# Layer 2 image scores: from 96 small products of their own to four columns of the score products

## The reference

```python
q    = heads(x @ W_q);  k_t = heads(text @ W_k);  v_t = heads(text @ W_v)       # text: 252 tokens
probs_t     = softmax(q @ k_t^T * scale);  text_out = probs_t @ v_t
k_ip = heads(ip @ W_k_ip);  v_ip = heads(ip @ W_v_ip)                           # ip: 4 tokens
attn_scores = q @ k_ip^T * scale                                                # (16, 20, 256, 4)
qsem  = l2norm(probs_t @ text);  sem = qsem @ l2norm(ip)^T
fused = attn_scores + 0.5 * sem
ip_out = (softmax(fused) * spatial_mask) @ v_ip
out = (text_out + ip_out) @ W_out + b_out + x
```

## Time and profile before

| | us |
|---|---|
| median of 3 runs | 1647.1 |
| lowest, highest | 1647.05, 1652.91 |
| the profiled execution | 1653.22 |
| its span, first to last instruction | 1651.4 |

### The profile page before, as it was taken

One profiled execution on the slowest core, in us unless ns is written; L12 is line 12 of the kernel. 1 busy time (PEld: TensorE's weight loads), 2 busy tenths in 40 slices (PEclk: granted clock), 3 DMA queues, 4 the chain that ended last, 5 costly groups with the idle time before them and its releaser, 6 DMA issues.

```text
span 1651.4 us, 42229 instructions
## 1 busy us (share of the span) xinstructions
PE 1586.4 (96%) x14152; PEld 1411.9 (85%) x14152; DVE 1388.2 (84%) x4113; ACT 991.9 (60%) x2044; POOL 716.0 (43%) x629
## 2 busy tenths in 40 slices
PE   6999999999999999999999999999999999999986
PEld 6888888888888888778788999999999999999965
DVE  4688788888888888876879999999999999999985
ACT  3455555565655565554656666666666666666652
POOL 3234422222233322433556555555655555655441
PEclk9999999999999999997999999999999999999998
DMA  8334444443444444543233323332333323332211
GB/s 225 98 105 122 127 122 124 130 130 116 127 125 128 122 128 124 146 117 91 80 110 91 99 73 103 102 104 73 102 94 104 96 79 103 110 100 62 81 30 43
DMA packets 204224, 175.30 MB, mean 106 GB/s; under 512 B 45440, under 2 KB 203530, under 8 KB 204010
## 3 DMA queue, kind: packets, MB, share of 16 engines
q1 hardware_dynamic: 204010, 172.60, 36.3%
HBM read 112.13 MB, written 60.38 MB: 104 GB/s over the span
## 4 chain that ended last, share of the span: by engine, by line
PE 89%; DVE 5%; issue 2%; ACT 1%; DMA 1%; SPq 1%; DVEq 0%; POOL 0%; ACTq 0%; POOLq 0%
PE MISC L104 27%; PE GP L104 20%; PE NAT L287 10%; PE TR L300 8%; PE PV L346 5%; PE PV L331 4%; PE PV L328 3%; PE PV L349 2%; PE MISC L249 2%; PE MISC L390 1%; PE MISC L488 1%; DVE ZP L920 1%; DVE TMP L801 1%; PE MISC L389 1%; PE MISC L410 1%
## 5 line engine op out<-in xcount | busy, mean ns | idle before, releaser
L1013 POOL TENSOR_TENSOR ZS<-ZP 128x256 f32<-128x256 f32 x267 | 279.8, 1048 | 295.7 <-DVE ZP L920 294.0
L562 ACT ACTIVATE P<-TA 128x512 f32<-128x512 f32 x320 | 202.3, 632 | 280.7 <-DVE TA L913 279.3
L287 PE MATMUL NAT<-KS,QS 65*128 65x256 f32 x1280 | 300.5, 317 | 3.1 <-DMA KS<-qk_parts 1.6
L930 DVE SCALAR_TENSOR_TENSOR PM<-P,PH 128x512 f32<-128x512 f32 x320 | 269.1, 841 | 0.0
L104 PE MATMUL GP<-PH,GH 128*128 128x256 f32 (+1 forms) x960 | 249.1, 289 | 18.0 <-DVE ZP L920 16.1
L300 PE MATMUL TR<-QS,KS 69*128 69x256 f32 (+1 forms) x1280 | 260.4, 285 | 6.0 <-DMA QS<-max_rows 4.5
L805 DVE TENSOR_REDUCE MX<-NAT 128x2 f32<-128x504 f32 x320 | 216.0, 675 | 44.2 <-PE NAT L287 39.5
L287 PEld LDWEIGHTS NAT<-KS,QS 65*128 65x128 f32 x1280 | 201.5, 192 | 56.6 <-issue 41.9
L104 PE MATMUL GP<-PH,GL 128*128 128x256 f32 (+1 forms) x960 | 243.1, 281 | 0.0
L237 POOL TENSOR_TENSOR PARTS<-QKF,PARTS 112x508 fp32r<-112x508 f32 (+3 forms) x93 | 120.1, 1291 | 269.5 <-ACT PARTS L590 268.9
L565 ACT ACTIVATE P<-TR 128x512 f32<-128x512 f32 x320 | 192.5, 601 | 73.8 <-PE TR L300 70.8
(11 more groups left out here) (256 smaller groups left out, 3772.7 us busy)
## 6 DMA issues: line engine op xcount, KB each, us to landing
QS<-qk_parts SPq DMA_DIRECT2D x480, 64.0 KB
KS<-qk_parts SPq DMA_DIRECT2D x480, 64.0 KB
qk_parts<-PARTS SPq DMA_DIRECT2D x128, 224.0 KB, 2.9
CT<-in_ctx_t SPq DMA_DIRECT2D x32, 512.0 KB, 3.9
qk_parts<-PARTS SPq DMA_DIRECT2D x64, 192.0 KB, 2.4
XT<-in_x_t SPq DMA_DIRECT2D x48, 112.0 KB, 2.7
XT<-x_t SPq DMA_DIRECT2D x48, 112.0 KB, 2.3
XB<-in_x SPq DMA_DIRECT2D x16, 320.0 KB, 4.0
```

What stands on the lines that cost most here:

```text
L287: ins = e.matmul(NAT[s % 2][:, i * T:(i + 1) * T], QS[0:KQ, h, i * 128:(i + 1) * 128], KS[0:KQ, h, :], start=True, stop=True)
L562: e.activation(P[:, s % NP, :], TA[:, s % 2, :], ACT.Exp, scale=SCALE).then_inc(q["exp"], 1)
L930: e.scalar_tensor_tensor(PM[:, s % 2, :], P[:, (S1 + s) % NP, :], 2.0, PH[:, s % NS, :].bitcast(F32), ALU.mult, ALU.subtract).then_inc(q[" ...
L1013: e.tensor_tensor(ZS[s % NZ][:, :], ZP[:, s % 2, 0:S], ZP[:, s % 2, S:2 * S], ALU.add).then_inc(q["zs"], 1)
```

## The change

The image keys of the batch are copied by ACT from KIP into columns 252 to 255 of QKF and of PARTS's high part, two copies of 4 columns ahead of the two large ones, for each of the three channel groups. POOL subtracts over 512 columns in place of 508. The stacked keys therefore hold the image keys in the padding, and NAT holds the image scores in columns 252 to 255 of each half. ACT reads these 2 x 4 numbers of each partition out of NAT in every iteration from t = 310 on, scaled, into SC. PE waits for that read before it overwrites the bank. TR uses 124 key columns in its second half in place of 128, so the top partitions of that bank are set to zero once, in the last two steps of layer 1. Removed are the mask products on DVE, the six products and the scaling of slot 17, the mask's DMA, and the memset of the padding.

```diff
@@ PE @@
                 if s >= 2:
                     e.wait_ge(q["mx"], s - 1)
+                if s >= S1 + 2:
+                    e.wait_ge(q["sc"], s - S1 - 1)
                 for i in range(2):
                     ins = e.matmul(NAT[s % 2][:, i * T:(i + 1) * T], QS[0:KQ, h, i * 128:(i + 1) * 128],
                                    KS[0:KQ, h, :], start=True, stop=True)
...
-                w = TRK0 if b < B else TRK1
+                w, t1 = (TRK0, T) if b < B else (TRK1, NT)
                 for i in range(2):
-                    ins = e.matmul(TR[s % 2][:, i * S:(i + 1) * S], KS[0:w, h, i * 128:(i + 1) * 128],
+                    t_i = min((i + 1) * 128, t1)
+                    ins = e.matmul(TR[s % 2][0:t_i - i * 128, i * S:(i + 1) * S], KS[0:w, h, i * 128:t_i],
                                    QS[0:w, h, :], start=True, stop=True)
...
-                for i in range(2):
-                    for m, (_, mn) in enumerate(MT):
-                        w = mn // 4
-                        ins = e.matmul(k[:, i * 80 + m * 28:i * 80 + m * 28 + w], QKF[0:mn, m, i * 128:(i + 1) * 128],
-                                       KBD[0:mn, m, 0:w // 4, :], start=True, stop=True)
-                ins.then_inc(q["scm"], 1)
@@ ACT, after the exponential and PH of iteration t @@
+            s = t + LEAD - 1 - S1
+            if 0 <= s < S1:
+                b, h = divmod(s, H)
+                if s == 0:
+                    e.wait_ge(q["pv"], G1 - NGRP)
+                if h == 0 and b >= 3:
+                    e.wait_ge(q["fu"], 8 * (b - 3) + 2)
+                e.wait_ge(q["mx"], S1 + s + 1)
+                e.mul(SC[:, b % 3, :, NI * h:NI * h + NI], NAT[s % 2][:, :].rearrange("p (a t) -> p a t", a=2)[:, :, NT:T], SCALE).then_inc(q["sc"], 1)
...
+                        ip = KIP[0:mn, m, NI * (b - B):NI * (b - B) + NI]
+                        e.copy(QKF[0:mn, m, w:S + T], ip)
+                        e.copy(QKF[0:mn, m, 0:w], k[0:mn, 0:w])
+                        e.copy(PARTS[0:mn, m, 0, w:S + T], ip)
+                        e.copy(PARTS[0:mn, m, 0, 0:w], k[0:mn, 0:w]).then_inc(q["qk_hi"], 1)
...
-                e.mul(SC[:, b % 3, :, :], ring.bank["scm", b][:, 0:160].rearrange("p (a n) -> p a n", a=2), SCALE).then_inc(q["sc"], 1)
@@ DVE @@
-                e.wait_ge(q["sc"], b + 1)
+                e.wait_ge(q["sc"], H * (b + 1))
...
-                e.tensor_tensor(KBD[0:112, 0:2, :, :], KMASK[0:112, :, :].unsqueeze(1).broadcast_to([112, 2, 8, 4]),
-                                own[0:112, 0:2, :].unsqueeze(2).broadcast_to([112, 2, 8, 4]), ALU.mult).then_inc(q["kbd"], 1)
...
-                e.tensor_tensor(TA[:, s % 2, :], TR[s % 2][:, :], ST[:, b % 2, :], ALU.add).then_inc(q["sum"], 1)
+                ins = e.tensor_tensor(TA[:, s % 2, :], TR[s % 2][:, :], ST[:, b % 2, :], ALU.add)
+                if s >= S1 - 2:
+                    ins.then_inc(q["tail"], 1)
+                    e.wait_ge(q["tail"], s - S1 + 3)
+                    ins = e.memset(TR[s % 2][96:128, S:2 * S], 0.0)
+                ins.then_inc(q["sum"], 1)
```

More of the change, by code:

```diff
@@ L44 @@
 AT1 = dict(q=(0, 4, 9), k=(1, 5, 10), spill=(2, 6, 11), x_in=-22, xts=-9, c_in=-15, ctn=-4, cts=-2, v=(6, 8), gr=(12, 13), gl=(13, 14),
-           kbd=9, scm=17, vip_in=38, vip=46, cmb=48, rs=((48, 49, 50, 51, 52, 53), (48, 49, 50, 51, 52, 53)), inv=56, f0=60, f2=61, sub=64, tx=65, sum=68, f1=71,
+           vip_in=38, vip=46, cmb=48, rs=((48, 49, 50, 51, 52, 53), (48, 49, 50, 51, 52, 53)), inv=56, f0=60, f2=61, sub=64, tx=65, sum=68, f1=71,
            ptt=72, hst=(74, 76), htl=(75, 77), om=(78, 82), y=(79, 83), out=84, xb_in=66)
@@ L53 @@
 WO_IN, WO_HI, WO_LO = S1 + 28, S1 + 32, S1 + 33
-MASKS_IN, SMALL, PADS, SEL_IN = S1 - 21, S1 - 19, S1 - 30, S1 - 16
+MASKS_IN, SMALL = S1 - 21, S1 - 19
 ONES_OF = (S1 - 18, S1 + 2)
@@ L160, in build @@
         sb, pair = tiles(second)
-        PH, KMASK, KBD = sb("PH", [128, NS, 2 * S], F32R), sb("KMASK", [128, 8, 4]), sb("KBD", [128, 3, 8, 4])
+        PH = sb("PH", [128, NS, 2 * S], F32R)
+        sb("in_wvi0", [128, 128])
         VMASK, E21 = sb("VMASK", [80, C]), sb("E21", [128, SLOT])
@@ L235, in parts_low @@
     def parts_low(e, b, m):
-        mn, w = MT[m][1], S + T if b < B else S + NT
-        e.tensor_tensor(PARTS[0:mn, m, 1, 0:w], QKF[0:mn, m, 0:w], PARTS[0:mn, m, 0, 0:w].bitcast(F32), ALU.subtract).then_inc(q["qk_lo"], 1)
+        mn = MT[m][1]
+        e.tensor_tensor(PARTS[0:mn, m, 1, :], QKF[0:mn, m, :], PARTS[0:mn, m, 0, :].bitcast(F32), ALU.subtract).then_inc(q["qk_lo"], 1)
     @block.tensor
@@ L583, in _ @@
                             e.wait_ge(q["tl"], b)
-                        else:
-                            e.wait_ge(q["scm"], b - B)
+                        if b == B:
+                            e.wait_ge(q["once_s"], 2)
                     if b:
@@ L588, in _ @@
                     e.wait_ge(q["qk"], 3 * b + m + 1)
-                    e.copy(QKF[0:mn, m, 0:w], k[0:mn, 0:w]).then_inc(q["qk_f"], 1)
-                    e.copy(PARTS[0:mn, m, 0, 0:w], k[0:mn, 0:w]).then_inc(q["qk_hi"], 1)
+                    if b < B:
+                        e.copy(QKF[0:mn, m, 0:w], k[0:mn, 0:w]).then_inc(q["qk_f"], 1)
+                        e.copy(PARTS[0:mn, m, 0, 0:w], k[0:mn, 0:w]).then_inc(q["qk_hi"], 1)
+                    else:
+                        ip = KIP[0:mn, m, NI * (b - B):NI * (b - B) + NI]
+                        e.copy(QKF[0:mn, m, w:S + T], ip)
+                        e.copy(QKF[0:mn, m, 0:w], k[0:mn, 0:w])
+                        e.copy(PARTS[0:mn, m, 0, w:S + T], ip)
+                        e.copy(PARTS[0:mn, m, 0, 0:w], k[0:mn, 0:w]).then_inc(q["qk_hi"], 1)
             b = of1(t, AT1["sub"])
@@ L884, in _ @@
                                 RZ[:, :, :].unsqueeze(3).broadcast_to([128, 2, H, D]), ALU.mult).then_inc(q["tx"], 1)
[L885 to L893, removed]
-                e.tensor_tensor(KBD[0:112, 0:2, :, :], KMASK[0:112, :, :].unsqueeze(1).broadcast_to([112, 2, 8, 4]),
-                                own[0:112, 0:2, :].unsqueeze(2).broadcast_to([112, 2, 8, 4]), ALU.mult).then_inc(q["kbd"], 1)
-                e.tensor_tensor(KBD[0:96, 2, :, :], KMASK[0:96, :, :], own[0:96, 2, :].unsqueeze(1).broadcast_to([96, 8, 4]),
-                                ALU.mult).then_inc(q["kbd"], 1)
             b = of1(t, AT1["ctn"])
@@ L1048, in _ @@
             if b is not None:
+                if b == 0:
+                    e.wait_ge(q["w1_m"], 16)
                 e.wait_ge(q["vip_in"], 16 * (b + 1))
@@ L1076, in _ @@
                 e.tensor_tensor(WO[1][0:CK, :, :], WOR[1][0:CK, :, :], WO[0][0:CK, :, :].bitcast(F32), ALU.subtract).then_inc(q["w1_lo"], 1)
[L1077 to L1080, removed]
             if t == SMALL:
                 e.wait_ge(q["vm"], 3 * B)
-                e.memset(KBD[:, :, :, :], 0.0).then_inc(q["ready"], 1)
                 e.memset(E21[:, :], 0.0).then_inc(q["ready"], 1)
-                e.wait_ge(q["ready"], 2)
+                e.wait_ge(q["ready"], 1)
                 e.memset(E21[:, 21:22], 1.0).then_inc(q["ready"], 1)
@@ L1183, in _ @@
                 if b < 2:
-                    e.wait_ge(q["ready"], 4)
+                    e.wait_ge(q["ready"], 3)
                 if b:
```

5 lines of the change are left out of this document (1 added, 4 removed).

## The result

The changed kernel takes 1664.7 us (median of 4 runs, 1662.2 to 1669.6) where the kernel before takes 1650.0 beside it (4 runs, 1647.1 to 1654.0): ratio 1.0091, 95% interval 1.0055 to 1.0127, so 14.7 us slower. A later measurement of both gave 1.0098 (1.0075 to 1.0122). The profiled execution took 1669.62 us with a span of 1667.8, against 1653.22 and 1651.4 before: +16.4 us, where the prediction summed +15.

The account below looks back on a forecast made before the run. PE was taken to set the pace, DVE close behind. Steady batches +3.5, end of layer 1 +8 and first batches +3.5 summed to +15 us, giving 1662 us; range 1643 to 1676.

Parts of the forecast that it names:

- The mechanism: PE's next NAT waits for ACT's small read, queued behind the exponential and PH; 1662 us, chance 0.62.
- Rival B: Reads come early enough that PE never waits and DVE becomes the bound: 11.5 us less, 1636; chance 0.12.
- Rival C: Cheaper restart and ends, early batches absorb lateness: steady -2, early +1, end of layer 1 +4, 1650; chance 0.18.
- the end of layer 1: Iterations 311 to 319 take 2.8 us each through the new wait, delaying NAT of 321: +8 us, bounds +4 to +11.
- Rival D: Each small operation costs as much as the 160 column read, 0.30 us: steady +10, end +10, early +5, 1672; chance 0.08.
- The loop's links: TR to exponential 0.44 us, to PH 0.68, then 0.52, read 0.19, to PE 0.10: TR to NAT 1.93 us.
- Slot 17: Steady batch, where the products are removed: NAT waits for the read, so 0.39 us gained and not 1.36.
- Slot 2: Steady batch: exponential already late behind ACT's copies, tiny copies add 0.15 us; loss of 0.48 us with PE's restart.
- Slot 14: Short slot of a steady batch: read through at 1020.04 against NAT at 1019.97; loss of 0.1 us with the restart.
- The other slots: Remaining slots of a steady batch: covered by PE's own products, with 0.08 us loss for the closest.
- The first batches: Start of layer 2, short and long iterations alternate, late at 322, 342, 362: +3.5 us, bounds 1 to 6.
- The last iterations: End of the kernel: also has short iterations, but DVE's ZP holds them anyway; 0.

Follow-up runs that it names:

- the opened one: Changed kernel with ACT's small read placed ahead of the exponential instead of behind PH: 0.9944 of the kernel before, 1643.8 us.
- the doubled read: Changed kernel with a second small read of the same 8 columns, to a scratch tile, ahead of the real one: 1.0172 of the kernel before.
- the kernel with f1=70: Kernel before with one offset changed, DVE's two masked products issued in slot 10 in place of slot 11: 0.9964 of the kernel before.

## Why the prediction was right

**The mechanism: right.** The wait was where it was said, ACT's share of the chain rose, and taking the loop apart took the loss away (1.0098 to 0.9944). Rival B fell with the changed kernel and came true in the opened one. Rival C asked for cheaper ends; the end of layer 1 was dearer (+10.8 for its +4). Its steady part of -2 us was about as near to the measured 0 as my +3.5. Rival D fell with the doubled read.

**The loop's links.** TR to NAT measured 1.96 us for 1.93 + 0.03. The read lasts 0.171 us (0.19; my own slope gives 0.196), and from its start to NAT 0.32 us pass, as predicted for the two links with the start (0.19 + 0.10 + 0.03). I weighed the Trainium skill's 0.3 us budget (ScalarE: Activation LUTs, rules for kernel authors) and passed it over; the 0.171 us bear that out. The budget is given for an activation whose bias is a pointer operand, which I had left out. Another section of the Trainium skill's page (ScalarE: Activation LUTs, What ACT_TABLE_LOAD costs) has a fixed 186 ns for an activation with immediate scale and bias; with 8 elements that is an estimate of 0.19 us, which is closer. The Trainium skill lets successive activations overlap by about 93 ns. The trace agrees: the two reads above last 0.17 us each and start 0.07 apart, so they overlap by 0.10.

**The terms of the sum.**
- Slot 17: gain 0.39 predicted, 0.37 measured. Slot 2: loss 0.48, measured 0.52; the two tiny copies delay the exponential by 0.19 us and not 0.15. Slot 14: 0.10, measured 0.08. (With the restart of 0.1 us that slot 2 has in the working, slot 14 would be 0.17; the term was not worked out alike.)
- The other slots: 0.08 predicted. Measured +0.21 in slot 11 (copies ahead of the exponential as in slot 2, which I had not walked through), +0.06, +0.02, and gains of 0.06, 0.08 and, in slot 12, 0.37. I had POOL's longer subtraction at nothing and did not look at what its start moves on DVE. The steady sum was +0.27 and came out at 0.0: two misses of opposite sign; over all of them +0.2 and +0.3 us came in place of +3.5.
- The end of layer 1: +8 predicted, +10.8 measured in both profiles from NAT of 310 to NAT of 321. The first step was right: NAT of 311 comes 2.75 us behind NAT of 310, and the walk had 730.6 - 727.83 = 2.77. A loop at full clock takes 2.79 to 2.83 us, as forecast (2.8). What was too small lies behind that. At the low clock (0.52 and 0.50, with 1.2 GHz as the level) a loop takes 3.12 to 3.17: NAT to the maximum is 0.87 us there and 0.58 at full clock. Iterations 311 to 314 take 13.0 us together, 1.8 more than four such loops, for the 2.5 that I had for the Gram halves. Iterations 318 and 319 take 3.54 and 3.52 and have the memsets, which I had at nothing and which stand in the chain: 757.93 - 757.62 = 0.31 us each. Iteration 317, with value products of layer 1 in it, takes 3.84. Iteration 320 takes 2.91 in place of my 2.3, but PE waits for nothing at its end, and it took 2.92 before: its projections at the low clock set it, not the loop. The bound that I had given for the lower clock, +11, was the better number.
- The first batches: +3.5 with bounds 1 to 6; +9.4 in one profile, +1.9 in the other. The first of them takes 60.5 us and not 63.1 even in the kernel with f1=70, whose edit acts from iteration 390 on, behind it. One profile can't size this term.
- The last iterations: 0 predicted, -1.9 and -2.0 in the two profiles. The losses of the loop are there (iterations 620, 621, 624 and 625 take 2.3 us for 1.4 to 1.7), but 622 takes 2.6 for 3.8, and 626 and 627 take 5.1 together for 8.7. What holds them before was not followed up, and the gain is not firm: with the tiny copies moved and the read in the same place, 622 takes 3.94 and 627 takes 4.19 again.

**A check that missed.** ACT's busy time rose by 29.5 us and not by some 50: I had added whole durations, and the small operations overlap their neighbours by about 0.1 us each.

In the sum +15 stood against +14.7 and +14.9 in the medians. The loop was foreseen, the closeness was luck: steady batches too dear by some 3.3, the end of layer 1 too cheap by 2.8, the last iterations off by 2, and a term for the first batches that two profiles put at 9.4 and 1.9.

## What to carry to other kernels

- Before moving work to an engine with idle time, ask what stands ahead of it in that engine's order and whether that waits for the engine you relieve. A read of 0.17 us at the end of an iteration tied NAT to TR and cost 25 us (good to some 5) against the same read at the start.
- Work that is taken off the bounding engine uncovers waits; follow the next one (here ZP on DVE) before counting the gain. 1.36 us of products a batch were worth 0.5.
- When a slot changes that the edit doesn't touch, look for short DVE operations that have become long beside a POOL operation; one digit in a schedule gave 0.36%.

## What the hardware showed that I had not expected

- A DVE operation of 80 columns and two SBUF inputs lasts 0.29 us, and 1.32 us when a POOL subtraction starts just ahead of it; DVE passes with one input in PSUM keep their 0.68 us beside the same subtraction.
- Two reads of 8 columns on ACT start 0.07 us apart, though each is shown as 0.17 us long; a tiny copy of 4 columns, shown as 0.19 us long, puts off the operation behind it by 0.09 to 0.10 us.
- The lower clock lengthens a loop by far less than twice: 3.12 to 3.17 us for 2.8 at the end of layer 1, where NAT to the maximum, the part that PE sets, grows from 0.58 to 0.87.
